# A transformer layer with routed experts on one core: attention scores in four strips of the array, router logits with the router's weights stationary, and a new order of work

## The reference

```
h = take(weight, ids)                                  # (8, 1024, 256)
qkv = norm(h) @ Wqkv.T + bqkv                          # 16 heads of 16
p = softmax(q.k / 4) over the 8 positions of a column
h = h + (p v) @ Wo.T + bo
x = norm(h)
s = sigmoid(x @ Wg.T)                                  # 16 experts in 4 groups
choice: s + bias; best 2 groups by their best pair; best 4 experts in them
cw = 2.5 * s / sum(s over the 4), else 0
h = h + sum_e cw_e * relu(x @ W1_e.T)^2 @ W2_e.T + relu(x @ Ws1.T)^2 @ Ws2.T
```

## Time and profile before

| | |
|---|---|
| median of 3 runs | 1297.54 us (1296.45 to 1298.26) |
| the profiled execution | 1296.51 us, its span 1294.7 us |
| granted TensorE clock, mean | 0.995 |
| TensorE busy | 1259.3 us (97%) |
| VectorE busy | 1022.7 us (79%) |
| ScalarE busy | 591.2 us (46%) |
| POOL busy | 500.2 us (39%) |
| DMA | 91.66 MB, 71 GB/s |

### The profile page before, as it was taken

One profiled execution on the slowest core, in us unless ns is written; L12 is line 12 of the kernel. 1 busy time (PEld: TensorE's weight loads), 2 busy tenths in 40 slices (PEclk: granted clock), 3 DMA queues, 4 the chain that ended last, 5 costly groups with the idle time before them and its releaser, 6 DMA issues.

```text
span 1294.7 us, 19965 instructions
## 1 busy us (share of the span) xinstructions
PE 1259.3 (97%) x7556; PEld 1037.6 (80%) x7556; DVE 1022.7 (79%) x1732; ACT 591.2 (46%) x1040; POOL 500.2 (39%) x717
## 2 busy tenths in 40 slices
PE   4798999999999999999999999999999999999998
PEld 3467889797888979788797888979788797888987
DVE  4989787887878789787878878788787878978754
ACT  5234445444554544454353544544355354444443
POOL 6437254161623507253260724416262360705100
PEclk9899999999999999999999999999999999999999
DMA  6002222121321212122121322212122120212131
GB/s 217 1 17 83 66 83 82 35 82 49 99 66 55 94 33 97 52 83 82 34 86 45 100 66 82 71 46 82 50 89 76 51 92 29 94 49 83 66 107 57
DMA packets 34128, 91.66 MB, mean 71 GB/s; under 512 B 4720, under 2 KB 13296, under 8 KB 34032
## 3 DMA queue, kind: packets, MB, share of 16 engines
q1 hardware_dynamic: 30960, 81.99, 19.0%
q0 software_dynamic: 3072, 8.39, 2.5%
HBM read 81.46 MB, written 8.91 MB: 70 GB/s over the span
## 4 chain that ended last, share of the span: by engine, by line
PE 94%; DVE 3%; issue 1%; ACT 1%; POOL 1%; DMA 0%; DVEq 0%; POOLq 0%; SPq 0%
PE psY L1157 32%; PE psH L1142 30%; PE psB L1188 10%; PE psB L1203 9%; PE psA L1233 4%; PE psB L1221 2%; PE psA L1221 2%; PE psA L1245 2%; PE psB L1174 1%; PE psA L1174 1%; DVE ring L771 1%; PE psA L1254 1%; PE psY L1261 0%; DVE stats L754 0%; POOL xin L399 0%
## 5 line engine op out<-in xcount | busy, mean ns | idle before, releaser
L1157 PE MATMUL psY<-w_hi,hid_hi 128*128 128x256 f32 x1152 | 328.5, 285 | 0.0
L1157 PE MATMUL psY<-w_hi,hid_lo 128*128 128x256 f32 x1152 | 324.5, 282 | 0.0
L1157 PE MATMUL psY<-w_lo,hid_hi 128*128 128x256 f32 x1152 | 323.6, 281 | 0.0
L733 DVE SCALAR_TENSOR_TENSOR r_sb<-psH,cwB 128x512 f32<-128x512 f32 x256 | 174.8, 683 | 113.7 <-PE psH L1142 102.9
L533 ACT ACTIVATE hid_hi<-r_sb 128x512 fp32r<-128x512 f32 x288 | 179.8, 624 | 181.4 <-PE psY L1157 181.4
L1157 PEld LDWEIGHTS psY<-w_hi,hid_hi 128*128 128x128 f32 x1152 | 217.3, 189 | 31.4 <-issue 23.5
L1142 PE MATMUL psH<-xT_hi,w_hi 128*128 128x512 f32 x576 | 229.2, 398 | 1.4 <-DVE r_sb L733 1.4
L1142 PE MATMUL psH<-xT_hi,w_lo 128*128 128x512 f32 x576 | 227.4, 395 | 0.0
L1142 PE MATMUL psH<-xT_lo,w_hi 128*128 128x512 f32 x576 | 227.3, 395 | 0.0
L531 ACT ACTIVATE p_sb<-r_sb 128x512 f32<-128x512 f32 x288 | 180.2, 626 | 101.8 <-DVE r_sb L733 94.6
L1157 PEld LDWEIGHTS psY<-w_lo,hid_hi 128*128 128x128 f32 x1152 | 216.9, 188 | 8.1
(11 more groups left out here) (136 smaller groups left out, 1980.6 us busy)
## 6 DMA issues: line engine op xcount, KB each, us to landing
cwB<-cw_dram SPq DMA_DIRECT2D x128, 512.0 KB, 3.9
out<-h SPq DMA_DIRECT2D x32, 256.0 KB, 3.2
xin<-table,idx POOLq DMA_INDIRECT x64
ring<-w_t SPq DMA_DIRECT2D x4, 256.0 KB, 5.3
h<-w_t SPq DMA_DIRECT2D x2, 512.0 KB, 8.5
ring<-w_t SPq DMA_DIRECT2D x1, 512.0 KB, 5.9
p_sb<-w_t SPq DMA_DIRECT2D x2, 256.0 KB
cwB<-w_t SPq DMA_DIRECT2D x1, 512.0 KB
```

Source lines behind the costliest of these rows:

```text
L733: nc.vector.scalar_tensor_tensor(r_sb[:, n % 2, :], psH[:, n % 2, :], 0.0, cwB[:, (r // QN) % 2, r % QN, :], ALU.max, ALU.mult).then_inc(w ...
L1157: last = nc.tensor.matmul(psY[:, j // 2, (j % 2) * D:(j % 2 + 1) * D], hid[a][:, e % R, j * P:(j + 1) * P], W2[b][:, e, :], start=(e == 0 ...
```

## The change

Three things are changed.

1. Scores. `product` t is now half t % 2 of positions t // 2, so two neighbouring products are the two halves of the same positions. `score(b, lp)` waits for both and issues four matmuls to the strips 0, 32, 64 and 96. A group in the period is now two such calls, of the same four products' amount as before.
2. Logits. The router's weights, high and low, and the first 96 columns of the output projection's weights lie side by side and are the stationary operand (128 columns); x moves, 512 columns, in 4 matmuls. The first 32 partitions of the result are the logits, transposed. ScalarE copies them out to `cwT` (`logits_out`, new), TensorE transposes them back in 4 transposes (`logits_back`, new) into the other half of `psA`, and `router` copies from there.
3. The order of the steps is written anew on all four engines, in the prologue and in the period. The number of `warm` calls is 17 in both.

```diff
-        WO = [sb(f"wo_{p}", [P, KH, D], f32r) for p in ("hi", "lo")]
-        WG = sb("wg_hi_lo", [P, KH, 2, E], f32r)
+        WGO = sb("wg_hi_lo_wo_hi", [P, KH, 2 * E + D], f32r)
+        WO = [WGO[:, :, 2 * E:2 * E + D], sb("wo_lo", [P, KH, D], f32r)]
...
-            lp, ih = t % LP, t // LP
+            lp, ih = t // KH, t % KH
...
+            def logits_out(blk):
+                act.wait_ge(logit_mm, nth(blk, 1, 1))
+                wait(act, cwT_stored, nth(blk, 16, 0))
+                nc.scalar.copy(cwT[:, :], psA[0:2 * E, 0, :]).then_inc(lgT_ready, 1)
+
             def router(blk):
-                act.wait_ge(logit_mm, nth(blk, 1, 1))
+                act.wait_ge(lg_back, nth(blk, 1, 1))
...
-                               psA[:, 0, 0:TT * 2 * E]).then_inc(lg_ready, 1)
+                               psA[:, 1, 0:TT * 2 * E]).then_inc(lg_ready, 1)
...
-            def score(blk, t):
+            def score(blk, lp):
...
+                for ih in range(KH):
+                    pe.wait_ge(prod_ready[ih], nth(blk, LP, lp + 1))
...
+                for ih in range(KH):
+                    for li in range(2):
+                        row = 64 * ih + 32 * li
+                        last = nc.tensor.matmul(psB[row:row + 32, 0, :], head_sum[:, lp, :],
+                                                ring[:, (KH * lp + ih) % 4, li, :],
+                                                start=(lp == 0), stop=(lp == LP - 1))
+                    last.then_inc(score_mm, 1)
...
             def logits(blk):
...
+                for kh in range(KH):
+                    for a in range(2):
+                        last = nc.tensor.matmul(psA[:, 0, :], WGO[:, kh, 0:P], x[a][:, kh, :],
+                                                start=(kh == 0 and a == 0), stop=(kh == KH - 1 and a == 1))
+                last.then_inc(logit_mm, 1)
+
+            def logits_back(blk):
+                pe.wait_ge(lgT_ready, nth(blk, 1, 1))
...
+                    last = nc.tensor.transpose(psA[:, 1, j * 2 * E:(j + 1) * 2 * E], cwT[:, j * P:(j + 1) * P],
+                                               ident[0:2 * E, 0:2 * E])
+                last.then_inc(lg_back, 1)
```

More of the change, by code:

```diff
@@ L569, in weights_out @@
                 act.wait_ge(cwT_mm, nth(blk, 1, 1))
-                nc.scalar.copy(cwT[:, :], psA[0:E, 1, :]).then_inc(cwT_ready, 1)
+                nc.scalar.copy(cwT[0:E, :], psA[0:E, 1, :]).then_inc(cwT_ready, 1)
             def exponent(blk):
@@ L921, in period @@
                 if b < B:
+                    hidden_lo(b, 2)
                     weigh(b, 4)
@@ L931, in period @@
                 if b < B:
-                    hidden_lo(b, 4)
+                    weigh(b, 5)
                 if b + 1 < B:
@@ L935, in period @@
                 if b < B:
+                    hidden_lo(b, 4)
                     weigh(b, 6)
+                    hidden_lo(b, 5)
+                    weigh(b, 7)
                 if b + 1 < B:
@@ L939, in period @@
                 if b < B:
-                    weigh(b, 7)
-                    hidden_lo(b, 5)
                     weigh(b, 8)
@@ L948, in period @@
                     hidden_lo(b, 6)
+                    weigh(b, 9)
+                    hidden_lo(b, 7)
                 if b + 2 < B:
@@ L951, in period @@
                 if b < B:
-                    weigh(b, 9)
-                    hidden_lo(b, 7)
+                    weigh(b, 10)
                     hidden_lo(b, 8)
@@ L957, in period @@
                 if b < B:
-                    weigh(b, 10)
-                    hidden_lo(b, 9)
                     weigh(b, 11)
-                    weigh(b, 12)
                 if b + 2 < B:
@@ L964, in period @@
                 if b < B:
+                    hidden_lo(b, 9)
                     hidden_lo(b, 10)
@@ L1005, in period @@
                 if b + 1 < B:
-                    route(b + 1, 10)
+                    route(b + 1, 9)
+                if b < B:
+                    hidden_lo(b, 13)
+                    weigh(b, 15)
+                if b + 1 < B:
+                    route(b + 1, 10)
+                if b < B:
+                    hidden_lo(b, 14)
+                if b + 1 < B:
+                    route(b + 1, 11)
+                    route(b + 1, 12)
                 if b < B:
@@ L1018, in period @@
                     route(b + 1, 16)
+                if b < B:
+                    weigh(b, 17)
+                if b + 1 < B:
                     route(b + 1, 17)
@@ L1200, in score @@
                     pe.wait_ge(qkv_ready, nth(blk, 6, 5))
-                for li in range(2):
-                    row = 64 * ih + 32 * li
-                    last = nc.tensor.matmul(psB[row:row + 32, 0, :], head_sum[:, lp, :], ring[:, t % 4, li, :],
-                                            start=(lp == 0), stop=(lp == LP - 1))
-                last.then_inc(score_mm, 1)
+                for ih in range(KH):
[5 more added lines that the diff above has]
+                    last.then_inc(score_mm, 1)
             def spread_probs(blk, t):
@@ L1295, in period @@
                 if b < B:
+                    up(b, 8)
+                    down(b, 4)
+                    up(b, 9)
+                    down(b, 5)
                     up(b, 10)
[L1297 removed]
                 if b + 1 < B:
                     out_projection(b + 1)
[L1300 to L1301 removed]
                 if b < B:
@@ L1330, in period @@
                     score(b + 2, 1)
+                if b < B:
+                    down(b, 10)
+                    up(b, 15)
+                    down(b, 11)
+                    up(b, 16)
+                    down(b, 12)
+                if b + 2 < B:
                     score(b + 2, 2)
@@ L1410, in _ @@
             score(1, 0)
+            transpose_rows(1, 0)
             score(1, 1)
             score(1, 2)
+            logits(0)
+            logits_back(0)
+            qkv(1, 5)
+            warm(4)
             score(1, 3)
-            score(1, 4)
-            score(1, 5)
-            transpose_rows(1, 0)
-            score(1, 6)
-            score(1, 7)
-            logits(0)
             warm(4)
             up(0, 0)
-            qkv(1, 5)
             warm(4)
             up(0, 1)
+            weights_transpose(0)
+            warm(4)
             up(0, 2)
-            warm(4)
-            weights_transpose(0)
             spread_probs(1, 0)
```

302 lines of the change are left out of this document (134 added, 168 removed).

## The result

The changed kernel takes 1312.11 us (median of 4 runs, 1307.11 to 1314.24) against 1297.9 us for the kernel before it on the same chip (1296.45 to 1298.79). The ratio is 1.0105, interval 1.0074 to 1.0136: **slower by 1.05%**, where I had forecast 1249.6 us, 3.7% faster. The profiled execution of the changed kernel took 1311.46 us, with a span of 1309.3.

The account below looks back on a forecast made before the run. TensorE, never waiting in the loop, was taken as the bound; 14 x (3.44 + 0.32 - 0.35) plus 0.3 for the last logits saved 48.0 us, giving 1249.6 us as the median, range 1240 to 1270.

Parts of the forecast that it names:

- The order must keep it fed: Loop queues: with TensorE's own work at 73.3 us a period, the new order must feed it with 3.8 us less slack.
- the softmax: VectorE's queue in the loop: reduction starts 0.7 us late, probabilities done 19.3 us behind up 14, TensorE there after 19.6.
- the second spread: TensorE in the loop: waits until ScalarE has copied the expert weights out of the same PSUM partitions, done 0.3 us late.
- 0.35 us of new waiting a period, ends 0 and 3: TensorE's new waits in the loop from the new order, taken off the savings in each of 14 periods.
- both savings: TensorE's work in a loop period: 3.44 us less for scores and 0.32 us less for logits.
- The rival that ended slower: Loop from softmax through expert weights, second spread and weigh 2 to up 4; at 5 us of waiting 1315 us; chance 0.02.
- my sign for a wrong order: Period over 74.5 us, TensorE idle before a spread row, released by VectorE's probabilities or ScalarE's cwT.
- Scores: TensorE's score groups: four strips at the pace of pairs, 1.72 + 0.12 us instead of 3.56, 3.44 us less a period.
- Logits: TensorE's router logits: 1.79 us removed, 0.93 for four matmuls and 0.54 for transposes back added, 0.32 us saved a period.
- So no stall there if my overlap is right: First spread of the next block: no TensorE stall if VectorE's neighbouring instructions overlap, 2 us if there is none.
- The copy of the expert weights: ScalarE's copy, now behind the next block's relu and both squares: done 0.3 us after TensorE reaches the second spread.
- The prologue, where I took 0 with ends of 4: Before the loop: second product waits for a later qkv result, last scores end sooner; net 0, ends -4 and +4 us.

Follow-up runs that it names:

- e9: e1 with both halves' scores written to the same two strips in the loop; 1303.55 us, ratio 1.0047.
- e6: e1 with the old logits (16 matmuls that move 32 columns, no copy out, no transposes back); 1260.10 us, ratio 0.9715.
- e11: e8 with the period before the last laid out for its missing work (up 13, down 10 earlier, transposes back later); 1249.76 us, ratio 0.9639.
- e8: e7 with ScalarE's copy of the expert weights one place earlier, ahead of the next block's first square; 1253.81 us, ratio 0.9658.
- e1: The changed kernel with POOL's gather ahead of `root_of_sum` again, in the period only; 1257.13 us, ratio 0.9697 to the kernel before.
- e5: e1 with the four products of each loop score group given out half by half, in the old order; 1266.96 us, ratio 0.9767.
- e12: e1 with POOL held by 19 linked products of a spare tile behind `root_of_sum`, rows still early; 1271.74 us, ratio 0.9806.
- e4: The changed kernel, gather late, with the experts' add ahead of `norm_stats` and `norm_stats` moved behind hidden_lo 3; 1287.24 us, ratio 0.9925.
- e7: e1 with the gather ahead of `root_of_sum` in the prologue too; 1257.93 us, ratio 0.969.

## Why the prediction was wrong

**The step that failed** is the one that begins "The order must keep it fed": "I walked the new queues with the durations of the rows." I walked three of the four queues. The two tight places that I named, the softmax and the second spread, were looked for along TensorE's waits; POOL, busy in 39% of the span, was taken as idle enough, and no row of its queue stands in my prediction. The term was "0.35 us of new waiting a period, ends 0 and 3"; it measured 36.9 / 13 = 2.84 us of standing and 1.42 us of slower work, 4.3 us, and both savings were gone. A walk of it would have taken three lines: `root_of_sum` now waits until VectorE comes to the low halves of the probabilities; the gather behind it lasts 5.2 us, and its landing 4 to 7; `norm_stats` is seven VectorE instructions behind those same low halves. So VectorE stands for the rows in every period of the loop, by 73.1 / 15 = 4.9 us on the mean of all 15 waits. What I had was the wrong habit: I asked of each moved step how late it would be, and not what it was now in front of.

**The rival that ended slower** had the right shape and the wrong place: a loop that closes once a period and costs TensorE what it is late, deciding at 3.76 us a period. I put it at softmax, expert weights and weigh 2. It was sum of weights, gather, `norm_stats`, add. I gave such a case 0.02. That its 1315 us is near the 1312 measured is luck: it is what 5 us of waiting would cost, and no wait of that loop was long. Nor did my sign for a wrong order point there: I had said idle time in front of a spread, and it was in front of `down` 0. Nothing in the old trace pointed at the gather, whose waits there are 2.9 us in all; only the comparison of the orders did.

**What held**, by the runs in which the gather is early:
- Scores: 1.85 us a group against 1.84; 46.4 us of time in the undoing (e9) against 48. The Trainium skill (TensorE: Matmul & The Clock Gate, section "Part 3: Packing small matmuls") has 2.38 times for three column tiles, which would be 2.28 us a group by my estimate of 0.54 us a quartet. The trace does not bear out that use of the figure: four strips go at the pace of two. No run here has one strip or three.
- Logits: 0.93 as forecast. The transposes back 0.36 and then 0.20 at the expert behind them, 0.56 together, against 0.54. In time 3.0 us against 4.8 (e6), in the period 0.30 against 0.32; part of the difference is the wait in the last period but one, which I had overlooked and e11 removes.
- The softmax: in the changed kernel `s_max` starts at 635.41, 0.8 us after the last score record ends (634.60), where I had 0.7, and the first spread at 643.07, right behind the matmul before it. "So no stall there if my overlap is right": right.
- The copy of the expert weights: "done 0.3 us after TensorE is there". The spread took 0.74 in place of 0.46, and e8 shows it as time, 4.1 us. This 0.28 us a period is what the term of 0.35 was meant for.
- The period without the gather's fault: 73.82 us, against 73.66.

**What was 7.5 us too good even then** (e1 against the forecast; 7.1 in the spans). The loop: 13 x 0.16 = 2.1. The prologue, where I took 0 with ends of 4: both kernels reach the loop's first score group at 154, but e1 has done one `up` and one `down` fewer by then, 2.8 us of work; why they get less done by then stays open. The groups from 0 to 154 us (before, then e1):

```profile
L1142 PE MATMUL psH<-xT_hi,w_hi 128*128 128x512 f32 x32 | 13.3, 416 | 1.4 <-DVE r_sb L733 1.4
...
L1157 PE MATMUL psY<-w_hi,hid_hi 128*128 128x256 f32 x44 | 12.4, 282 | 0.0
```

```profile
L1156 PE MATMUL psH<-xT_hi,w_hi 128*128 128x512 f32 x30 | 12.2, 405 | 0.0
...
L1171 PE MATMUL psY<-w_hi,hid_hi 128*128 128x256 f32 x40 | 11.2, 281 | 0.0
```

(Two such records are an `up`, four a `down`.) And the end, where the work of block b + 2 is missing that keeps TensorE fed in the loop: 1.8 us of standing for the normed rows and for the copy of the logits. I had walked the loop's period only. Together 6.7 of 7.1.

## What to carry over

When an order is laid out anew, walk every queue, the least busy one first: an in-order queue is late by its latest step, and a step with 40 us of room has none once it stands behind a step that waits for the end of the period. For each pair of steps that changed places, ask what the one now in front waits for and who wants the one behind. Walk the first and the last periods too, in which the work is missing that covers the waits in the loop.

An engine that is busy 38% of the time can cost more than the one that is busy 97%: here one exchange of two lines on POOL was worth 55 us, more than the 48 that the whole change was to gain.

## Of the hardware, not expected

- A quartet of fp32 matmuls of 32 columns keeps the pace of a pair, 0.43 us, in all 14 periods, and so does a queue in which neighbours share a strip (e5, 1.98 us a group against 3.56 with two strips in e9). The same section of the Trainium skill says that matmuls start and end strictly in the order of the program; by that, as an estimate, three pairs of records of e5's first half would have to start before the fourth and the second half could, and the group would take (3 + 4) x 0.43 + 0.12 = 3.1 us. Its 1.98 us and its starts in fours show that here different strips don't wait for each other.
- POOL's indirect DMAs hold its queue: four of them 5.2 us in the period shown, 0.95 to 1.23 each and 0.30 between them. From the start of the last one to the landing it was 4.0 us in one period, 6.6 in the next and 2.8 in a later one.
- In the changed kernel's loop, 10 of the 12 stands of TensorE before `down` 0, 2.6 to 3.9 us each, lie in periods with a mean granted clock of 0.98, though TensorE is busy on both sides of them; the periods with the other two (2.7 and 1.1 us) have 1.00. This slower work costs 1.42 us a period. In the loops of e12 and e4, where no single stand is above 1.0 us (13 us and 21 us in all), the clock is 1.00.
- A VectorE instruction of 128x64 values took 2.30 us in the place of 0.23 while a POOL instruction of 128x1024 values ran beside it, once each in e7, e8 and e11. What the two share is open.
